# Sequence-convolution and adapter kernel: half of the rounded strip copied on chip, strips in five buffers, a shorter parameter stage and a spread load order

## The reference, cut to what matters

```python
# x: (128, 32, 512); itok_B_78_3631: lengths; itok_B_6_15: adapter ids (all in the 0..31 range)
dt = exp(log_dt); A = -exp(log_A_real) + 1j * A_imag; dtA = A * dt[:, None]
K = 2 * einsum('hn,hnl->hl', C * (exp(dtA) - 1) / A, exp(dtA[:, :, None] * arange(512))).real   # (32, 512)
y = irfft(rfft(x, 1024) * rfft(K, 1024))[..., :512] + x * D[:, None]     # causal convolution, per head
x = x + y * (arange(512) < length)
# rows of x in the order (batch, head), ids per batch:
x = x + x @ W.T + bias + (x @ A_w[id].T) @ B_w[id].T                     # W: 512 x 512, rank 16, 32 adapters
```

## Time and profile before

| what | value |
|---|---|
| median of 3 runs | 232.27 us (230.84 to 236.08) |
| the profiled execution's own time | 231.91 us |
| its span | 230.2 us |
| mean granted TensorE clock | 0.969 of full speed |
| DMA over the span | 56.46 MB, mean 245 GB/s |
| strip loads | 32 of 512 KB, median 5.6 us to landing |

### The profile page before, as it was taken

One profiled execution on the slowest core, in us unless ns is written; L12 is line 12 of the kernel. 1 busy time (PEld: TensorE's weight loads), 2 busy tenths in 40 slices (PEclk: granted clock), 3 DMA queues, 4 the chain that ended last, 5 costly groups with the idle time before them and its releaser, 6 DMA issues.

```text
span 230.2 us, 4329 instructions
## 1 busy us (share of the span) xinstructions
PE 196.4 (85%) x1046; PEld 168.2 (73%) x1046; DVE 176.1 (76%) x388; ACT 111.7 (49%) x321; POOL 87.5 (38%) x136
## 2 busy tenths in 40 slices
PE   0054797699495899996999999999999999999993
PEld 0042696699485799985888888888888888888882
DVE  4888677979787477737899988887878888787651
ACT  2725135144315333306767666656666666666410
POOL 4320002427323700041575464645445454545300
PEclk9999799799979999997999999999999999999999
DMA  5994999989999878792468776767677667763512
GB/s 126 336 404 147 336 272 367 402 281 357 398 384 396 310 259 277 272 324 96 138 183 274 255 223 209 219 206 214 223 206 213 203 225 205 229 197 125 182 48 91
DMA packets 26338, 56.46 MB, mean 245 GB/s; under 512 B 3859, under 2 KB 4307, under 8 KB 25939
## 3 DMA queue, kind: packets, MB, share of 16 engines
q1 hardware_dynamic: 22658, 47.78, 60.8%
q0 software_dynamic: 2560, 8.39, 12.1%
q10 hardware_dynamic: 1104, 0.13, 0.4%
HBM read 45.64 MB, written 10.65 MB: 245 GB/s over the span
## 4 chain that ended last, share of the span: by engine, by line
PE 72%; DMA 20%; DVE 5%; issue 1%; ACTq 0%; ACT 0%; SPq 0%; DVEq 0%
PE y_ps L866 39%; PE z_ps L829 18%; DMA strip<-k_pad 14%; PE z_ps L854 7%; PE y_ps L876 3%; PE y_ps L875 3%; DMA x_t<-x_tile 3%; DMA k_pad<-k_sb 2%; DMA par<-params 1%; PE k_ps L815 1%; DVE ex L532 1%; ACTq L450 0%; DVE a_raw L748 0%; DVE x_t L761 0%; DVE mag L537 0%
## 5 line engine op out<-in xcount | busy, mean ns | idle before, releaser
L866 PE MATMUL y_ps<-w_hi,xp 128*128 128x512 f32 x256 | 86.0, 397 | 0.0
L829 PE MATMUL z_ps<-xp,strip 128*128 128x512 f32 (+3 forms) x384 | 68.4, 339 | 14.0 <-DMA strip<-k_pad 13.7
L829 PEld LDWEIGHTS z_ps<-xp,strip 128*128 128x128 f32 x384 | 62.1, 201 | 20.2 <-DMA strip<-k_pad 15.5
L866 PEld LDWEIGHTS y_ps<-w_hi,xp 128*128 128x128 f32 x256 | 48.8, 191 | 10.3
L866 PE MATMUL y_ps<-w_lo,xp 128*128 128x512 f32 x128 | 51.1, 399 | 0.0
L349 POOL DMA_INDIRECT strip<-b_tab,b_idx x32 | 38.2, 1195 | 27.4 <-PE z_ps L829 17.6
L344 POOL CAST ag<-a_hl 128x128 fp32r x64 | 23.6, 370 | 47.8 <-PE z_ps L854 33.5
L376 ACT ACTIVATE xp<-z_all 128x512 fp32r<-128x512 f32 x32 | 19.8, 628 | 34.4 <-PE z_ps L829 27.7
L453 ACT ACTIVATE ag<-a_hl 128x64 fp32r x128 | 25.7, 249 | 20.3 <-issue 20.1
L748 DVE TENSOR_TENSOR a_raw<-y_ps,bias_sb 128x512 f32<-128x512 f32 x32 | 22.1, 689 | 13.7 <-issue 8.5
L660 DVE TENSOR_TENSOR z_all<-z_ps,mask 128x512 f32<-128x512 f32 (+2 forms) x33 | 22.2, 673 | 12.2 <-PE z_ps L829 12.0
(11 more groups left out here) (105 smaller groups left out, 165.8 us busy)
## 6 DMA issues: line engine op xcount, KB each, us to landing
strip<-k_pad SPq DMA_DIRECT2D x32, 512.0 KB, 5.6
z_all<-x_conv SPq DMA_DIRECT2D x16, 512.0 KB, 9.5
x_t<-x_tile SPq DMA_DIRECT2D x32, 256.0 KB
out<-a_raw SPq DMA_DIRECT2D x32, 256.0 KB
x_t<-b_rows SPq DMA_DIRECT2D x1, 1024.0 KB, 7.2
a_raw<-a_t SPq DMA_DIRECT2D x1, 1024.0 KB, 8.6
w_sb<-w_t SPq DMA_DIRECT2D x1, 1024.0 KB, 7.5
b_tab<-w_hi SPq DMA_DIRECT2D x1, 1024.0 KB, 11.6
```

Of the source, the lines that this page charges most:

```text
L829: last = nc.tensor.matmul(z_ps[:, h % ZS, m * P:L], strip[:, h % XS, t, m * P:(m + 1) * P], xp[:, h % XS, 0:LC - m, e, :], start=(n == 0), ...
L866: last = nc.tensor.matmul(y_ps[:, s % TS, :], xp[:, s % XS, c, e, :], w[:, c, :], start=(n == 0), stop=False)
```

## The change

1. **Strips.** The rounded row is read for 64 partitions of 576 columns into `strip_hi`; ACT copies columns 64 to 575 of partitions 0 to 63 to partitions 64 to 127 (`copy_down`). The remainder row still comes whole, by a DMA of its own, into `strip_lo`. Five buffers (`SS`) in place of four. PE waits for the copy and for the second DMA. The gathered B rows get a buffer of their own, in the space of the phase scratch (`work`).
2. **Order of loads on SP.** Seven pairs of x heads instead of eight ahead of the loop, the other heads one by one over heads 1 to 25; the tables a_t and w_t in quarters, `b_tab` stored in halves as soon as they are split, and the first four x tiles at heads 26 to 29.
3. **Parameter stage.** One term fewer in `exp`; the magnitudes of the first four heads made by ACT alone with `zr` as its scale, those of the other 28 later in one piece; one reciprocal of 64 columns for two of 32; small products moved from DVE to POOL; two pairs of DVE multiplies and adds joined; `split_x(0)` and `(1)` behind the first sine.
4. **Order on ACT, POOL and PE.** `SPLIT_B`, `SPLIT_A`, `SPLIT_W` at heads 5 to 8, 9 to 15, 22 to 25 (before 7, 11 and 18 onwards), group 3 of K after head 6 and not 7, the w_sb additions and splits of POOL interleaved by quarter, POOL's first gathers behind the last factors of K and no longer behind the last convolutions.

```diff
 XS = 4
+SS = 5
+HALF = P // 2
-PRE = 8
-X_AT = {3: 8, 5: 9, 7: 10, 9: 11, 11: 12, 13: 13, 15: 14, 17: 15}
-A_AT, W_AT = 5, 12
-SPLIT_B, SPLIT_A, SPLIT_W = 7, 11, 18
-K_AFTER = {2: 0, 3: 7, 4: 14}
+PRE = 7
+X_AT = {1: 14, 2: 15, 4: 16, 5: 17, 6: 18, 8: 19, 10: 20, 11: 21, 13: 22, 15: 23, 16: 24, 18: 25, 19: 26, 21: 27,
+        22: 28, 23: 29, 24: 30, 25: 31}
+A_AT = {3: 0, 5: 1, 7: 2, 9: 3}
+TAB_HI_AT, TAB_LO_AT = {12: 0, 14: 1}, {17: 0, 20: 1}
+W_AT = {18: 0, 19: 1, 21: 2, 22: 3}
+BIAS_AT = 24
+XT_AT = {26: 0, 27: 1, 28: 2, 29: 3}
+SPLIT_B = {5: 0, 6: 1, 7: 2, 8: 3}
+SPLIT_A = {9: 0, 11: 1, 13: 2, 15: 3}
+SPLIT_W = {22: 0, 23: 1, 24: 2, 25: 3}
+K_AFTER = {2: 0, 3: 6, 4: 14}
...
             def load_strip(h, s):
-                src = bass.AP(tensor=k_pad.tensor, offset=k_pad.offset + 2 * h * PAD + 1,
-                              ap=[[1, P], [PAD, 2], [1, L]])
-                sp.dma_start(strip[:, s, :, :].bitcast(F32), src).then_inc(strip_landed[s], 16)
+                row = k_pad.offset + 2 * h * PAD + 1
+                hi = bass.AP(tensor=k_pad.tensor, offset=row, ap=[[1, HALF], [1, HALF + L]])
+                lo = bass.AP(tensor=k_pad.tensor, offset=row + PAD, ap=[[1, P], [1, L]])
+                sp.dma_start(strip_hi[0:HALF, s, :].bitcast(F32), hi).then_inc(hi_landed[s], 16)
+                sp.dma_start(strip_lo[:, s, :].bitcast(F32), lo).then_inc(strip_landed[s], 16)
...
-                if h >= XS:
-                    sp.wait_ge(conv_done, h + 1 - XS)
-                load_strip(h, h % XS)
+                if h >= SS:
+                    sp.wait_ge(conv_done, h + 1 - SS)
+                load_strip(h, h % SS)
...
+            def copy_down(h):
+                act.wait_ge(hi_landed[h % SS], 16 * (h // SS + 1))
+                act.activation(strip_hi[HALF:P, h % SS, 0:L], strip_hi[0:HALF, h % SS, HALF:HALF + L].bitcast(F32),
+                               ACT.Copy).then_inc(hi_copied, 1)
...
+            for h in range(GROUPS[0][1]):
+                act.activation(mag[:, h, :], tab[:, 0:NL], ACT.Exp, scale=zr[:, h:h + 1]).then_inc(mags, 1)
...
+            copy_down(0)
+            copy_down(1)
             group_sines(2)
+            copy_down(2)
             for h in range(XS, NH):
...
+                copy_down(h - 1)
                 split_x(h)
...
-            exponents_of(0, GROUPS[1][1])
...
-                link(V.tensor_scalar(k, cs_x[:, 1, :], -0.25, None, ALU.is_lt))
-                V.scalar_tensor_tensor(cs_x[:, 0, :], k, -0.25, cs_x[:, 1, :], ALU.add, ALU.add).then_inc(angle_ready, 1)
...
-                link(V.tensor_scalar(ez[:, 0, :], th[:, :], -1.0, 1.0, ALU.mult, ALU.add))
-                link(V.reciprocal(ez[:, 1, :], ez[:, 0, :]))
-                link(V.scalar_tensor_tensor(ez[:, 2, :], th[:, :], 1.0, ez[:, 1, :], ALU.add, ALU.mult))
...
+            V.reciprocal(rr[:, :, :], rc[:, :, :]).then_inc(rec_ready, 1)
...
             fraction()
+            exponents_of(GROUPS[0][1], NH)
             remainder(0)
             multiply()
             scale()
-            exponents_of(GROUPS[1][1], NH)
...
             def head(h):
-                pe.wait_ge(strip_landed[h % XS], 16 * (h // XS + 1))
+                pe.wait_ge(strip_landed[h % SS], 16 * (h // SS + 1))
+                pe.wait_ge(hi_copied, h + 1)
...
-            for t in range(XT):
-                load_x_tile(t, t)
```

More of the change, by code:

```diff
@@ L34, with expm1_terms @@
 LN2_LO = math.log(2) - LN2_HI
+def expm1_terms(n):
+    pts = [math.log(2) / 2 * math.cos((2 * i + 1) * math.pi / (2 * n)) for i in range(n)]
+    div = [math.expm1(p) / p for p in pts]
+    for j in range(1, n):
+        for i in range(n - 1, j - 1, -1):
+            div[i] = (div[i] - div[i - 1]) / (pts[i] - pts[i - j])
+    poly = [div[-1]]
+    for i in range(n - 2, -1, -1):
+        poly = [(poly[k - 1] if k else 0.0) - (pts[i] * poly[k] if k < len(poly) else 0.0)
+                for k in range(len(poly) + 1)]
+        poly[0] += div[i]
+    return poly
+EXPM1 = expm1_terms(6)
 GROUPS = ((0, 4), (4, 8), (8, 16), (16, 24), (24, 32))
@@ L44 @@
 TS = 2
-BS = XS
+BS = 4
 OS = XS
@@ L92, in build @@
         mag = sb("mag", [P, NH, NL])
[L93 to L96, removed]
+        with nc.sbuf_tensor("work", [P, BS, G * (NA + NL)], F32) as work:
+            pass
+        b_hl = sb("b_hl", [P, BS, L], F32R)
+        uu, vv, xx, sines = (work[:, n, :].rearrange("p (h l) -> p h l", h=G) for n in range(BS))
         gg = sb("gg", [P, KS, G, NA])
-        g2 = sb("g2", [P, G, NA])
+        g2 = sb("g2", [P, G, 2, NA])
         ee = sb("ee", [P, KS, G, NC])
@@ L140, in build @@
         par_in, table_in, d_in, len_in, ids_in = (sem(n) for n in ("par_in", "table_in", "d_in", "len_in", "ids_in"))
-        w_in, a_in, b_in, bias_in, row_in = (sem(n) for n in ("w_in", "a_in", "b_in", "bias_in", "row_in"))
+        b_in, bias_in, row_in = (sem(n) for n in ("b_in", "bias_in", "row_in"))
+        w_in = [sem(f"w_in{n}") for n in range(NW)]
+        a_in = [sem(f"a_in{n}") for n in range(NW)]
         x_landed = [sem(f"x_landed{n}") for n in range(NH // XP)]
-        strip_landed = [sem(f"strip_landed{s}") for s in range(XS)]
+        strip_landed = [sem(f"strip_landed{s}") for s in range(SS)]
+        hi_landed = [sem(f"hi_landed{s}") for s in range(SS)]
+        hi_copied = sem("hi_copied")
         xt_landed = [sem(f"xt_landed{s}") for s in range(XT)]
@@ L284, in _ @@
             ai = par[:, 1, :]
+            turn = cs_x[:, 1, :]
             def twice(a):
@@ L326, in _ @@
                                 ALU.subtract).then_inc(a_split, 1)
-            pool.wait_ge(w_in, 16)
             for c in range(LC):
+                pool.wait_ge(w_in[c], 16)
                 d = w_sb[:, c, c * P:(c + 1) * P]
                 g.tensor_tensor(d, d, eye[:, :], ALU.add).then_inc(w_eye, 1)
[L331 to L337, removed]
+                pool.wait_ge(w_eye, c + 1)
+                if c == 0:
+                    pool.wait_ge(tab_lo_stored, 32)
+                if c:
+                    split_w(c - 1)
+            split_w(LC - 1)
             def gather(t, s):
@@ L376, in split_x, with magnitudes @@
                 act.activation(xp[:, h % XS, :, 0, :], z_all[:, h, :, :], ACT.Copy).then_inc(xc_hi_done, 1)
-            def magnitudes(n, h0, h1):
-                act.wait_ge(exponents, n)
+            def magnitudes(h0, h1):
+                act.wait_ge(exponents, 1)
                 act.activation(mag[:, h0:h1, :], mag[:, h0:h1, :], ACT.Exp).then_inc(mags, 1)
@@ L415, in _ @@
             group_sines(0)
+            split_x(0)
+            split_x(1)
+            group_store(0)
+            group_sines(1)
+            magnitudes(GROUPS[0][1], NH)
             split_x(2)
             split_x(3)
-            group_store(0)
-            group_sines(1)
-            magnitudes(2, GROUPS[1][1], NH)
             group_store(1)
+            copy_down(0)
+            copy_down(1)
             group_sines(2)
+            copy_down(2)
             for h in range(XS, NH):
@@ L529, in exp @@
                 link(V.tensor_scalar(ex_i[:, :], k, 127.0, 2.0 ** 23, ALU.add, ALU.mult))
-                link(V.tensor_scalar(q, r, 1 / 5040, None, ALU.mult))
-                for n in range(6, 0, -1):
-                    link(V.scalar_tensor_tensor(q, q, 1 / math.factorial(n), r, ALU.add, ALU.mult))
+                link(V.tensor_scalar(q, r, EXPM1[-1], None, ALU.mult))
+                for term in EXPM1[-2::-1]:
+                    link(V.scalar_tensor_tensor(q, q, term, r, ALU.add, ALU.mult))
                 return V.scalar_tensor_tensor(dst, q, 1.0, ex_i[:, :].bitcast(F32), ALU.add, ALU.mult)
@@ L827, in head @@
                 for n, (m, t, e) in enumerate(terms):
-                    last = nc.tensor.matmul(z_ps[:, h % ZS, m * P:L], strip[:, h % XS, t, m * P:(m + 1) * P],
+                    part = (strip_hi, strip_lo)[t]
+                    last = nc.tensor.matmul(z_ps[:, h % ZS, m * P:L], part[:, h % SS, m * P:(m + 1) * P],
                                             xp[:, h % XS, 0:LC - m, e, :], start=(n == 0), stop=(n == len(terms) - 1))
```

161 lines of the change are left out of this document (94 added, 67 removed).

## The result

The changed kernel takes 244.53 us in the median of 4 runs (244.09 to 247.55), 1.057 of the kernel before (95% interval 1.051 to 1.064): slower, where 220.4 was forecast, and outside the range. The profiled execution took 244.76 us with a span of 243.0.

The account below looks back on a forecast made before the run. Strip bytes on DMA were taken to bound the kernel up to 77.11 us, PE afterwards. Convolution, 70.0 us from 23.4, would end 11.1 us earlier, the tile start save 0.4: 231.9 - 11.1 - 0.4 = 220.4 us, range 214.5 to 227.

Parts of the forecast that it names:

- The sum: Convolution stage from 23.4 us: 65.3 + 1.7 + 1.5 + 1.5 = 70.0, ending 93.4 in place of 104.52; whole kernel 220.4 us.
- What bounds the kernel before: Strip landings, limited by DMA bytes, up to 77.11 us, then PE alone; tile stage untouched at 124 us.
- Start: Parameter stage: K's chain 2.0 us shorter, first strip issued 1.6 earlier, landing plus copy 0.3 longer; PE starts at 23.4.
- Bytes: Convolution stage: 26.4 MB falls to 23.2, 57 to 66 us of DMA against 65.3 of PE; DMA narrowly stops being the bound.
- Rival A: Half strip no cheaper to move, 64 partitions as slow as 128: 224.1 us, 218.6 to about 229; chance 0.30.
- ACT: Convolution stage: 32 copies of 0.63 us add 20 us to ACT's 26.2, hidden while strips land early.
- Slow clock: Convolution stage: one slow-clock stretch, at the first head, costing 1.7 us; three such stretches cost 5.1 before.
- Five buffers: Strips asked for four heads ahead, 7.8 us against 5.6 to land and 0.63 copy; 1.5 us wait left (0 to 6).
- Group 3: Group 3 of K one head earlier: crowded DVE delays PE's operand after head 6, 1.5 us PE wait (0 to 4).
- Rival B: Strip loop (landing, copy, convolution) lengthens: landing 11.9 gives 2.9 us a head, stage 93, 243 us; chance 0.08.

Follow-up runs that it names:

- a3_wide: Changed kernel with the rounded strip read for all 128 partitions of 576 columns (288 KB, not 144), copy kept: 239.23 us, 1.033.
- c2_ports: Changed kernel with the same 64 rows landed on partitions 32 to 95, two quarter copies, one on ACT, one on DVE: 241.09 us, 1.043.
- e3_low_order: Changed kernel, rows still on partitions 0 to 63, copy behind next head's rounding, groups 3 and 4 after heads 8 and 15, ids and splits moved: 239.89 us.
- e2_ports_act: Same order as `e3_low_order`, but rows landed on partitions 32 to 95, with two 32-partition copies, both on ACT: 232.50 us, 1.001.
- f1_ports_k7: `e2_ports_act` with group 3 of K after head 7, not 8: 231.49 us, 0.997.
- e4_whole_order: Same order as `e3_low_order`, but whole rounded strips and no copy: 230.75 us, 0.996.
- d1_late: Changed kernel with ACT copying strip h - 2 behind the rounding for head h, not strip h - 1 ahead of it: 241.49 us, 1.040.
- b5_wide: Kernel before, four buffers, with rounded rows as their own DMA onto all 128 partitions (288 KB) plus the copy on ACT: 245.71 us, 1.064.
- a2_k7: Changed kernel with group 3 of K after head 7 as before, not after head 6: 243.32 us, 1.047.
- c3_g3: Changed kernel with group 3 after head 7, ids at head 12, B splits at heads 8 to 11, A splits at 12 to 15: 243.59 us, 1.049.
- f2_whole_k7: `e4_whole_order` (whole strips, no copy) with group 3 of K after head 7, not 8: 228.12 us, 0.983.

## Why the prediction was wrong

- **The sum**, term by term: the stage took 93.75 us where 70.0 was the sum. PE waited 0.77, 7.94 and 1.86 us for groups of K, 10.6 where 1.5 stood; 8.8 us for strips where 1.5 stood; and was busy 74.4 us where 65.3 + 1.7 = 67.0 stood. These three make up the 23.7 us. They say where PE lost the time, not what removing a cause gives back: that is what the runs are for.
- **What bounds the kernel before**: right. Strips, by DMA, up to 77 us. The tile stage stayed as it was, but for 1 us.
- **Start**: right in sum, 1.5 us at PE's first head (1.3 forecast), by two errors that cancel. K's first matmul came 1.3 us earlier and not 2.0: the reciprocal of 64 columns took 0.54, and two operations beside POOL's 0.5 and 0.6. The store, out of the x loads' way, took 3.60 us and not 4.93, so the first strip was issued 2.6 us earlier (20.71 to 18.07; 1.6 forecast). But from there to PE's first head it took 5.1 us where it had taken 4.0, 1.1 more and not 0.3.
- **Bytes**: the failed step. 23.2 MB was right (23.3), but "at 409 GB/s that is 57 us, at 331 / 0.94 = 352 GB/s 66 us" took the rate from transfers onto all partitions. With 144 of a strip's 400 KB landing on partitions 0 to 63 the full rate was 280 over the stage and 302 in the window shown, so DMA stayed the bound. `a3_wide` (more bytes, faster), `c2_ports` (same packets, other partitions) and the pair `e3_low_order` and `e2_ports_act` show it. It is worth 5.3 us by `a3_wide` and 7.4 by that pair, of the 24 by which the forecast missed. With the landing put right and a good order `f1_ports_k7` still took 231.5, so the steps on ACT, group 3 and the clock below failed too.
- **Rival A** named this cause, and its rule of the Trainium skill ("SBUF — State Buffer", the DMA port swizzle: partitions 0 to 63 reach half of the ports) agrees with what the runs show. Landings on 32 to 95 came near those on all partitions without reaching them: at full share 302 / 0.91 = 332 GB/s in `e2_ports_act`, against 353 / 0.98 = 360 in `e4_whole_order` in the same window and 284 / 1.02 = 278 in `e3_low_order`. It was given 0.30 and should have had more than the forecast: the trace's silence on such a landing is no evidence against it. Its size was off too. It counted the half strip as 288 KB at the old rate, 224.1 us; but `a3_wide`, which moves just those 288 KB, runs 5 us faster than the changed kernel. So the rest of the queue pays as well. And of its signs only the low GB/s came as written: the share was 0.89, not 0.95, and PE waited for strips only from 82 us on, for groups of K before. In the packet records between 22 and 90 us, 2048-byte packets took 115 ns in the mean, 94 before and 89 in `a3_wide`.
- **ACT**: "hidden while strips land early" had its condition right and the check on it left out. The copy of strip h - 1 stands ahead of the rounding for head h, which is due when PE has finished head h - 4, two heads (3.9 us) after strip h - 1 was asked for; it landed in 7.5. Every late strip then delayed the rounding of x for the next head. Worth 3.0 us by `d1_late` here. With four buffers strip h - 1 is asked for one head later still, so the copy may well be most of the 13.7 us of `b5_wide`; no run shows that part alone.
- **Slow clock**: one stretch of 1.7 us was counted, PE lost 9.1 (74.4 less 65.3). Behind the gap at group 3 the granted clock was 0.51 from 50 to 56 us, and 0.57 from 110 to 114. The first two heads took 3.8 and 3.5 us and not 1.94 each; their matmuls took as long as those at 0.51, but the trace gives 1.00 for that stretch, so what slowed them is open.
- **Five buffers**: the margin was worked out for PE's use of the strip (7.8 us), not for the copy's, which comes two heads sooner.
- **Group 3**: seen, mis-sized. 1.5 us with bounds 0 and 4; PE waited 7.94. ACT's sine for the group waits for DVE, DVE's remainder for ACT's rounding behind it, and both stand behind a strip (the copy at 37.74 had waited 2.22 us for it). Loosening it alone showed next to nothing (`a2_k7`, `c3_g3`), which fits transfers as the bound; in the whole-strip kernels the order of groups, ids and splits was worth 6 us (234.1 to 228.1).
- **Rival B** gave 243 us for a landing of 11.9 and a head of 2.9 us; 244.5 and 93.75 / 32 = 2.9 were measured. As a mean that is luck: the median landing was 7.5 us, and 10.6 us of the stage are waits for groups of K. From 82.35 to 109.32 it holds: nine heads in 27.0 us, 3.0 each, with landings of 12.05 and 12.61 on the chain. There the DMA engines are full (1.06), so the long landing is rival A's slow queue seen from the strip's loop; which of the two to name was not tested.

Not settled: four against five buffers, and two DMAs a head against one, were not tried alone (with five buffers two DMAs a head can't cost much, since `f2_whole_k7` has them and is the fastest). The parts above come from kernels that share only some of the rest and don't sum exactly. No version came near 220.4: the best, with all the bytes and no copy, took 228.1.

## What to carry to other kernels

Before halving a transfer's partitions, ask where it lands: here 64 partitions from 0 slowed every transfer in the queue, so that twice the rows on 128 partitions ran faster (239.2 us against 244.5), and 64 partitions from 32 did so far less. A DMA share near 1 with GB/s below what full share moved before is the sign. An on-chip copy that replaces bytes belongs in the queue where its source has already landed, behind what the next head needs, and its engine must have the room: here even well placed it only drew level, and the same reordering with whole transfers won 1.7%.

## What the runs showed that I had not expected

A 64 by 512 copy on ACT takes as long as one of 128 by 512 (0.629 us on line 443, 0.629 on line 451), as the forecast had taken it without a row, and one of 32 by 512 does too (0.628 in `e2_ports_act`), so two quarter copies cost twice one half copy. Halving a load's rows did not shorten its landing: half strips took 7.5 us, as long as the 256 KB ones behind them. That is time in a full queue rather than the side they land on, for in `f1_ports_k7` it is 4.7 beside 5.1. In the changed kernel:

```profile
strip_lo<-k_pad SPq DMA_DIRECT2D x32, 256.0 KB, 7.7
...
strip_hi<-k_pad SPq DMA_DIRECT2D x32, 144.0 KB, 7.5
```
